# The first y0: two adjacency rows as whole fp32 products, scaled in the accumulators

## What is computed

```python
def _L0_gnn_ref(x, adj, weight, bias):
    y = jnp.einsum('nm,bmf->bnf', adj, x)
    y = y + x
    y = jnp.einsum('bnf,fo->bno', y, weight) + bias
    norm = jnp.sqrt(jnp.sum(y * y, axis=2, keepdims=True))
    return y / jnp.maximum(norm, 1e-12)
...
x = _layernorm(x + _L0_gnn_ref(x, adj, ...), axis=-1)
x = _layernorm(x + _L1_gnn_ref(x, adj, ...), axis=-1)   # masked attention
x = _layernorm(x + _L2_gnn_ref(x, adj, ...), axis=-1)   # gated relation layer
x = _layernorm(x + _L3_gnn_ref(x, adj, ...), axis=-1)   # Chebyshev layer
```

## Time and profile before

| | |
|---|---|
| median of three timed executions | 658.12 us |
| the profiled execution: its own time | 658.38 us |
| its span, first to last instruction | 656.2 us |
| TensorE busy | 629.6 us (96%) |
| VectorE busy | 567.4 us (86%) |
| ScalarE busy | 400.3 us (61%) |
| GpSimd busy | 74.1 us (11%) |
| mean granted TensorE clock | 0.996 of full |

### The profile page before, as it was taken

One profiled execution on the slowest core, in us unless ns is written; L12 is line 12 of the kernel. 1 busy time (PEld: TensorE's weight loads), 2 busy tenths in 40 slices (PEclk: granted clock), 3 DMA queues, 4 the chain that ended last, 5 costly groups with the idle time before them and its releaser, 6 DMA issues.

```text
span 656.2 us, 17523 instructions
## 1 busy us (share of the span) xinstructions
PE 629.6 (96%) x7443; PEld 487.4 (74%) x7443; DVE 567.4 (86%) x1512; ACT 400.3 (61%) x706; POOL 74.1 (11%) x50
## 2 busy tenths in 40 slices
PE   8899989999999999999999999999999999889994
PEld 3456767698678966799667976689667986549894
DVE  6889597889998999889899899889898898989635
ACT  6979572455946579274964659365893649432522
POOL 0114010020003100210002200021002100020002
PEclk9999999999999999999999999999999999999998
DMA  8710000000000200002000200002000000000012
GB/s 337 260 65 2 1 1 1 1 34 2 2 2 1 66 2 1 1 2 66 2 1 1 67 1 1 2 3 66 1 1 2 17 19 1 1 1 2 2 34 65
DMA packets 12445, 18.74 MB, mean 29 GB/s; under 512 B 592, under 2 KB 9040, under 8 KB 12368
## 3 DMA queue, kind: packets, MB, share of 16 engines
q1 hardware_dynamic: 12368, 17.63, 8.1%
HBM read 13.44 MB, written 4.19 MB: 27 GB/s over the span
## 4 chain that ended last, share of the span: by engine, by line
PE 62%; DVE 23%; ACT 7%; issue 4%; POOL 1%; DMA 1%; SPq 0%; ACTq 0%; DVEq 0%; POOLq 0%
PE r L1304 13%; PE r L1306 13%; PE r L1305 13%; DVE att L901 4%; PE r L1352 4%; DVE p_lo L906 4%; ACT att L412 3%; PE av L1467 3%; DVE stats L582 2%; PE r L1310 2%; ACT p_hi L291 2%; PE av L1476 2%; PE m L1304 2%; PE m L1305 2%; PE m L1306 2%
## 5 line engine op out<-in xcount | busy, mean ns | idle before, releaser
L248 POOL TENSOR_TENSOR small<-small,minus_half 128x8 f32<-128x8 f32 (+1 forms) x40 | 69.0, 1729 | 570.3 <-DVE small L609 308.9
L901 DVE TENSOR_TENSOR att<-att,adjT 128x1024 f32<-128x1024 f32 x64 | 77.9, 1219 | 11.3 <-ACT att L414 11.2
L412 ACT ACTIVATE att<-r,coef 128x1024 f32<-128x1024 f32 x64 | 70.4, 1101 | 21.5 <-PE r L1306 20.9
L1304 PE MATMUL r<-xq,a_hi 128*128 128x128 f16 x448 | 76.0, 219 | 0.0
L1305 PE MATMUL r<-xq,a_hi 128*128 128x128 f16 x448 | 76.0, 219 | 0.0
L1306 PE MATMUL r<-xq,a_lo 128*128 128x128 f16 x448 | 76.0, 219 | 0.0
L1304 PE MATMUL r<-rs,a_hi 128*128 128x128 f16 x448 | 75.9, 219 | 0.0
L1305 PE MATMUL r<-rs,a_hi 128*128 128x128 f16 x448 | 75.8, 219 | 0.0
L1306 PE MATMUL r<-rs,a_lo 128*128 128x128 f16 x448 | 75.8, 219 | 0.0
L414 ACT ACTIVATE att<-att 128x1024 f32<-128x1024 f32 x64 | 67.7, 1057 | 2.0
L906 DVE SCALAR_TENSOR_TENSOR p_lo<-p_hi,att 128x1024 f16<-128x1024 f16 x48 | 58.4, 1219 | 0.0
(11 more groups left out here) (423 smaller groups left out, 2110.7 us busy)
## 6 DMA issues: line engine op xcount, KB each, us to landing
adjT<-in_adj_t SPq DMA_DIRECT2D x8, 512.0 KB, 8.5
x<-in_x SPq DMA_DIRECT2D x7, 512.0 KB, 4.8
out<-outb SPq DMA_DIRECT2D x7, 512.0 KB, 3.4
pq<-in_adj SPq DMA_DIRECT2D x2, 512.0 KB, 8.6
u<-in_adj SPq DMA_DIRECT2D x2, 512.0 KB, 10.1
tmp<-in_adj SPq DMA_DIRECT2D x2, 512.0 KB, 10.5
x2s<-in_adj SPq DMA_DIRECT2D x2, 512.0 KB, 9.7
outb<-in_x SPq DMA_DIRECT2D x1, 512.0 KB, 11.8
```

What stands on the lines that cost most here:

```text
L248: return nc.gpsimd.tensor_tensor(dst, src, minus_half[:, 0:src.shape[-1]], ALU.pow)
L412: nc.scalar.activation(att[:, s], dst[:], ACT.Tanh, scale=c_tanh).then_inc(S["th"], 1)
L901: tt(att[:, s], att[:, s], adjT[:, t, :], ALU.mult).then_inc(S["pm"], 1)
L1304: mm(dst, s_hi, m_hi, start=start, stop=False, skip_group_check=True)
```

## The change

- TensorE multiplies chunks 0 and 1 (`RAW = 2`) as whole fp32 products of the unscaled features `x0` and `adjT`, four matmuls of 128 x 512 into `r1`, as soon as the chunks have landed. They stand where ten `keep_busy` products stood.
- The sum in `r1` is then multiplied in place by `x_up` = `xinv` x `ADJ_UP`: half 0 by ScalarE, half 1 by VectorE. The loop goes on with chunks 2 to 7 as before and adds the identity products of chunks 0 to 2 at chunk 2.
- The fp16 parts of chunks 0 and 1 are still needed later. GpSimd scales `adjT[0]` and `adjT[1]` in place by `ADJ_UP`, then makes `a_lo[0]` and `a_lo[1]` by a subtraction. ScalarE makes `a_hi[0]` first as before and `a_hi[1]` after chunk 7. `loop_blocks` on TensorE waits for GpSimd's two low parts.
- The transfer of the first weights goes behind chunk 2 instead of chunk 0. The product of q and k moves from chunk 1 to chunk 3, its copy on ScalarE from chunk 2 to chunk 4, `first_max` from chunk 4 to 5, `weights_sum` from chunk 6 to 7, and `x0_max(1)` behind `y0_lo`. ScalarE makes `y0_hi` before `scale_adj`, and scales chunks 0 and 1 later, behind batch 1's first `y0_hi`.

```diff
+RAW = 2
...
             for c in range(C):
                 sp.dma_start(adjT[:, c, :], adj_t[chunk(c)]).then_inc(adj_in[c], 16)
-                if c == 0:
+                if c == RAW:
                     sp.dma_start(xas[1][:, 0:4], w_first).then_inc(S["wq_in"], 16)
...
+            pool.wait_ge(S["raw_mm"], 2)
+            pool.wait_ge(S["adj_hi"], 1)
+            for c in range(RAW):
+                nc.gpsimd.tensor_scalar(adjT[:, c], adjT[:, c], ADJ_UP, None, ALU.mult).then_inc(S["adj_s"], 1)
+            for c in range(RAW):
+                pool.wait_ge(S["adj_s"], c + 1)
+                pool.wait_ge(S["adj_hi"], 1 if c == 0 else C + 1)
+                nc.gpsimd.tensor_tensor(a_lo[:, c], adjT[:, c], a_hi[:, c], ALU.subtract).then_inc(S["adj_lo_p"], 1)
...
-            for c in range(C):
+            def row_hi(c):
                 act.wait_ge(adj_in[c], 16)
+                copy(a_hi[:, c], adjT[:, c], ADJ_UP).then_inc(S["adj_hi"], 1)
+
+            row_hi(0)
+            first_x0_hi(0)
+            first_x0_hi(1)
+            for c in range(RAW, C):
                 if c < C - 1:
-                    copy(a_hi[:, c], adjT[:, c], ADJ_UP).then_inc(S["adj_hi"], 1)
+                    row_hi(c)
                 else:
+                    act.wait_ge(adj_in[c], 16)
                     for h in range(2):
                         copy(a_hi[:, c, half(h)], adjT[:, c, half(h)], ADJ_UP).then_inc(S["adj_hi"], 1)
-                if c < 2:
-                    first_x0_hi(c)
-                if c == 2:
+                    act.wait_ge(S["adj_s"], RAW)
+                    copy(a_hi[:, 1], adjT[:, 1]).then_inc(S["adj_hi"], 1)
+                if c == RAW:
+                    act.wait_ge(S["raw_mm"], 1)
+                    act.wait_ge(S["x_up"], 1)
+                    copy(r1[:, half(0)], r1[:, half(0)], x_up[:]).then_inc(S["raw_a"], 1)
+                if c == 4:
                     act.wait_ge(S["m_mm"], 1)
                     copy(m_sb, m7[:, 2 * P:3 * P]).then_inc(S["m_cp"], 1)
...
                 for c in range(first, last_):
-                    act.wait_ge(S["adj_lo"], c + 1 if c < C - 1 else C + 1)
-                    copy(adjT[:, c], adjT[:, c], LO_UP * P_UP).then_inc(S["adj_up"], 1)
+                    if c < RAW:
+                        act.wait_ge(S["adj_lo_p"], c + 1)
+                    else:
+                        act.wait_ge(S["adj_lo"], c + 1 - RAW if c < C - 1 else C + 1 - RAW)
+                    copy(adjT[:, c], adjT[:, c], LO_UP * P_UP / (ADJ_UP if c < RAW else 1.0)).then_inc(S["adj_up"], 1)
...
-                scale_adj(0, 3)
                 y0_hi(0, 0, r1[:, half(0)])
                 y0_hi(0, 1, r1[:, half(1)])
+                scale_adj(RAW, 3)
                 degrees(0, 3)
...
                 y0_hi(1, 0, m7[:])
+                scale_adj(0, RAW)
                 norm(0, 0, xas[0], V_CHUNKS)
...
+            dve.wait_ge(S["x_st"], 5)
+            ts(x_up[:], xinv[:], ADJ_UP, None, ALU.mult).then_inc(S["x_up"], 1)
...
-            for c in range(C):
+            first_x0_lo(0)
+            first_x0_lo(1)
+            dve.wait_ge(S["raw_mm"], 2)
+            dve.wait_ge(S["x_up"], 1)
+            ts(r1[:, half(1)], r1[:, half(1)], x_up[:], None, ALU.mult).then_inc(S["raw_d"], 1)
+            for c in range(RAW, C):
                 parts = [slice(0, N)] if c < C - 1 else [half(0), half(1)]
                 for n_, part in enumerate(parts):
-                    dve.wait_ge(S["adj_hi"], c + 1 + n_)
+                    dve.wait_ge(S["adj_hi"], c + n_)
                     stt(a_lo[:, c, part], adjT[:, c, part], ADJ_UP, a_hi[:, c, part], ALU.mult,
                         ALU.subtract).then_inc(S["adj_lo"], 1)
-                if c < 2:
-                    first_x0_lo(c)
-                if c == 4:
+                if c == 5:
                     first_max()
...
-                x0_max(1)
                 weights_split(0)
                 rows = Rows(0)
                 rows.begin()
                 y0_lo(0, 0, r1[:, half(0)])
                 y0_lo(0, 1, r1[:, half(1)])
+                x0_max(1)
                 dve.wait_ge(S["bc_in"], 16)
                 rows.y_half(0, r1[:])
...
             keep_busy(9)
             pe.wait_ge(S["x_max"], 1)
             mm(m7[:, 4:5], ones[:], xmax[:], start=True, stop=True).then_inc(S["x_sum"], 1)
-            pe.wait_ge(S["ident_ok"], 3)
-            keep_busy(10)
+            pe.wait_ge(S["x0_in"], 16)
+            for c in range(RAW):
+                pe.wait_ge(adj_in[c], 16)
+                for h in range(2):
+                    l_ = mm(r1[:, half(h)], x0[:, c], adjT[:, c, half(h)], start=(c == 0), stop=(c == RAW - 1))
+                    if c == RAW - 1:
+                        l_.then_inc(S["raw_mm"], 1)
...
             def loop_blocks():
 
+                pe.wait_ge(S["adj_lo_p"], RAW)
                 for h in range(2):
...
-            for c in range(C):
-                if c == 1:
+            pe.wait_ge(S["iu_ok"], 1)
+            for c in range(RAW, C):
+                if c == 3:
                     pe.wait_ge(S["wq_in"], 16)
                     pe.wait_ge(S["x_st"], 1)
                     mm(m7[:, 2 * P:3 * P], qT, kT, start=True, stop=True).then_inc(S["m_mm"], 1)
-                if c == 6:
+                if c == C - 1:
                     weights_sum(0, 0, 3)
-                if c in (0, C // 2):
-                    pe.wait_ge(S["x_lo"], 1 + 2 * c // C)
-                for h in range(2):
+                if c in (RAW, C // 2):
+                    pe.wait_ge(S["x_lo"], 1 + c // (C // 2))
+                for h in range(2):
+                    if c == RAW:
+                        pe.wait_ge(S[("raw_a", "raw_d")[h]], 1)
                     if h == 0 or c == C - 1:
-                        pe.wait_ge(S["adj_lo"], c + h + 1)
+                        pe.wait_ge(S["adj_lo"], c + h + 1 - RAW)
                     l_ = split_product(r1[:, half(h)], x0s[:, 0, c], x0s[:, 1, c], a_hi[:, c, half(h)], a_lo[:, c, half(h)],
-                                       c == 0, c == C - 1)
+                                       False, c == C - 1)
                     if c // (C // 2) == h:
-                        for part in range(2):
-                            l_ = mm(r1[:, chunk(c)], x0s[:, part, c], ident_up[:], start=False, stop=False, skip_group_check=True)
+                        for m in range(0 if c == RAW else c, c + 1):
+                            for part in range(2):
+                                l_ = mm(r1[:, chunk(m)], x0s[:, part, m], ident_up[:], start=False, stop=False, skip_group_check=True)
                     if c == C - 1:
                         l_.then_inc(S["y0_mm"], 1)
```

More of the change, by code:

```diff
@@ L159, in cd @@
             return ap.rearrange("p (c d) -> p c d", c=C)
+        x_up = sb("x_up", [P, 1])
         z_all = Stage(x3, xq, rs, pq, u, outb, r0)
@@ L164, in adj_resnorm @@
         names = ("w_in bc_in wq_in iu_ok x_in x1_in ident_ok const_ok m_cp w3_c m_mm w_max w_sum w_red w_ok wj_c "
-                 "dg_mm dg_hi dg_lo adj_hi adj_lo adj_up deg_ok sc_ok b3_ok "
+                 "dg_mm dg_hi dg_lo adj_hi adj_lo adj_lo_p adj_s adj_up raw_mm raw_a raw_d x_up deg_ok sc_ok b3_ok "
                  "norm_sq norm_r dis_ok x0_in x_max x_sum x_st x_hi x_lo "
```

## The result

The changed kernel takes 662.77 us (median of five executions, 662.35 to 665.67) against 658.12 for the kernel before on the same chip: a ratio of 1.0079, 95% interval 1.0057 to 1.0101. It is slower, inside the range, and 0.8 us less so than the 663.6 forecast. The profiled execution took 662.35 us, its span 659.8: the span grew by 3.6 us, what lies around it from 2.2 to 2.55.

A forecast was written before the change was run, and what follows sets the result against it. The bound was when VectorE begins y_half(0), at 23.69 us. GpSimd holding up VectorE's low parts was to delay it 5.45 us: 658.38 + 5.45 = 663.8 profiled, median 0.26 lower, 663.6 us; range 657.5 to 667.

The forecast's parts named there:

- The size of the hold: GpSimd beside VectorE's low parts: scaling 1.3 us, subtraction 2.4 us, each blocking throughout, together 7.4 us, between 5.5 and 10.
- with 10 it is +8: Upper bound: 10 us of GpSimd work beside VectorE's low parts would delay y_half(0) by 8 us.
- The walk: Timeline from chunk arrival to y_half(0), GpSimd and VectorE locking each other out both ways: y_half(0) at 29.15, +5.45 us.
- +0.15 without interference: Walk to y_half(0) with GpSimd not disturbing VectorE: start at 23.85 us, +0.15, TensorE's gain eaten by the later weights' sum.
- the mark: Start of VectorE's y_half(0), 23.69 us in the kernel before; whatever moves it was said to move all behind it.
- ScalarE costs nothing: ScalarE's two scalings before batch 0's norm, 1.97 us, fill 1.59 us idle; the 0.3 too much costs nothing.
- nothing gives the loss back: After y_half(0), the 5.45 us delay was to stay to the end, since TensorE is full behind 40 us.
- 29.5 when TensorE comes there: loop_blocks on TensorE: GpSimd's low parts done at 21.9 us, TensorE said to reach it at 29.5.
- Rival 1 (no lock): GpSimd beside VectorE's low parts costs little: +0.15 us, at most +1.3, 658.3, not slower; chance 0.28 shared with Rival 4.
- Rival 2 (no backlog): VectorE's last low part ends right after ScalarE's last copy, 18.0 instead of 19.05: -0.5 to -1.4, 657.2; chance 0.10.
- Rival 3: As forecast, but gaps in TensorE's loop drop its clock to 1.2 GHz, or GpSimd at upper bound: +8, 666.2; chance 0.14.
- Rival 4: Raw products hold TensorE past low part 2, ending after 11.2 us; time as in Rival 1, chance 0.28 shared with it.

The follow-up runs named there:

- before_with_gpsimd_reads: Kernel before plus two scalings and two subtractions on GpSimd, on buffers nobody reads, and two memsets filling these at the start; 664.95 us.
- memsets and filler: Changed kernel with two GpSimd memsets in place of its scalings and subtractions, and nine keep_busy products between raw products and loop; 659.14 us.
- memsets and no filler: Changed kernel with two GpSimd memsets of a_lo[0] and a_lo[1] (zeros) in place of its scalings and subtractions; 660.6 us.
- order_only: Kernel before with only the moves of the transfer, q and k product and copy, first_max, weights_sum and x0_max(1); 658.69 us.
- gpsimd_late: Changed kernel with GpSimd's four instructions waiting for VectorE's last low part and a_hi[1] behind y0_hi; 665.49 us.
- subtractions_behind_y0_lo: Changed kernel plus nine keep_busy products, ScalarE scaling chunks 0 and 1, copy and weights_sum moved, GpSimd only subtracting, after the first y0_lo; 660.2 us.
- subtractions_behind_split: Changed kernel plus nine keep_busy products, ScalarE scaling chunks 0 and 1, copy and weights_sum moved, GpSimd only subtracting, after the first weights' split; 658.6 us.
- before_with_four_scalings: Kernel before plus four idle GpSimd scalings of 128x1024 beside VectorE's low parts, on buffers nobody reads, no subtraction; 661.65 us.

## Why the prediction came out as it did

**Direction and mechanism: right.** GpSimd's instructions and VectorE's two-operand low parts keep each other out, in both directions. What was inferred from the roots' 2.54 against 1.64 us held for the direction that the trace before didn't show, as before_with_gpsimd_reads shows with no other engine's program changed. In both directions the one that comes second waits for the first: GpSimd through VectorE's instruction, VectorE through a part of GpSimd's.

**The size of the hold: the term that was off.** Predicted: scaling 1.3 us and subtraction 2.4 us, blocked for their whole length, 7.4 us in all. Measured: the scaling is much longer (2.8 us) and blocks much less (0.85 us, from when VectorE's instruction of that moment is over), the subtraction blocks 1.93 of its 2.12 us; 5.56 in all. The rule "blocked until the first has finished", which the prediction took from the Trainium skill, "SBUF — State Buffer", Who interferes with whom, holds for the subtraction to 0.2 us and not for the scaling. Had it held with the true lengths (2 x 2.8 + 2 x 2.12 = 9.8 us), the price would have been some 7.8 us by the prediction's own line ("with 10 it is +8"). Two errors in the scaling, length and share, partly cancelled: that is luck.

**The walk.** Low parts: predicted to end at 24.25, measured 23.26; the weights' sum read at 24.9, measured 23.18; `y_half(0)` at 29.15, measured 27.32. Of the 1.83 us between them, 1.0 is the earlier end of the low parts, most of it the shorter hold. Another 0.7 is that TensorE had the weights' sum (21.60) before the last low part: since subtraction 1 fell on the first half of part 7, and not on part 6, chunk 6 was through early. Part of the difference came back in the median by what the walk didn't have: 0.35 us more around the span, and a lower mean clock in some executions (0.993, 0.993 and 0.989 where the time is 662.8, 662.9 and 665.7, against 0.995 in the profiled one). So the median is 4.65 us behind, the span 3.6, and that the forecast of +5.45 came within 0.8 us of the median is in part luck.

**"+0.15 without interference": too low.** With memsets and filler the mark is at +1.15. Most of the 1.0 us between is the start of the loop: chunk 2 begins at 12.59 where the walk had 11.7, 0.7 of it because the raw products began at 1.2 GHz; the prediction had taken 2.4 GHz for all of them. (With memsets and no filler they ran at 2.4 GHz and chunk 2 began at 11.67, as walked, but then the loop itself ran at 1.2 GHz.) The second missing term is on ScalarE: the q and k copy behind chunk 4 waits for TensorE, and the high part of chunk 5 stands behind it. It shows as a gap of 0.24 us in TensorE's loop, before chunk 6 at 18.89, and as 0.3 us at the last low part in order_only. The prediction looked at what waits for the product, not at what queues behind the waiting copy. In the changed kernel low part 5 waits 0.34 us for the same reason.

**Behind the mark.** "ScalarE costs nothing" and "nothing gives the loss back" were right: 3.63 at the mark, 3.64 at the scores, 3.6 at the end. But "29.5 when TensorE comes there" for `loop_blocks` was wrong. TensorE begins them at 24.27 in the kernel before and at 28.38 in the changed one; it did no harm here, with GpSimd done at 22.11. The same mistake spoiled the expectation for gpsimd_late, and it cost 1.5 us between mark and scores in subtractions_behind_y0_lo, the lower clock included.

**Rival 1 (no lock)** is out: the low parts grow by up to 1.92 us. **Rival 2 (no backlog)** is nearly what subtractions_behind_split does, at no gain. **Rival 3**: by the mean clocks it may stand behind the 0.4, 0.6 and 3.3 us by which three executions lie above the fastest, but the profiled one doesn't show it (1.00 in all windows of 2 us read from 12 to 36 us). **Rival 4** is out: half 1 of the raw sum is read at 10.13.

## What to carry to other kernels

An idle engine isn't free help: before moving streaming work to GpSimd, list what VectorE runs beside it, and put the work where VectorE reads PSUM or one fp32 operand in a reduction, not beside instructions with two SBUF operands or a `tensor_scalar` from SBUF of more than one column; even a memset held such a `tensor_scalar` up. Then check who waits for the result and what stands behind that wait on its engine: moved late, the same two instructions cost 3 us and moved right, nothing. When an engine on the path is relieved, read from the trace how near the next one is; here VectorE got 1 us ahead of ScalarE and TensorE, and the time stayed the same.

## What the runs showed of the hardware

- A GpSimd `tensor_scalar` over 128x1024 fp32 takes 2.8 us and keeps a two-operand VectorE instruction out for 0.84 to 0.89 us; a `tensor_tensor` takes 2.12 and keeps it out for 1.93. If VectorE is in a low part when GpSimd starts, GpSimd waits for its end first (3.02 to 3.60 us for 2.8) and the hold counts from there. That the one with fewer operands is the longer was not expected. The Trainium skill, "GPSIMD Engine Reference", Performance versus the Vector engine, has 2.6 cycles an element for two inputs, an estimate of 2.2 us that the 2.12 bears out, and 1.03 for a body of up to two operations, an estimate of 0.9 us, a third of the 2.8 measured for the scaling, though near the time for which it holds VectorE.
- VectorE's `tensor_scalar` 128x128 fp32 to fp16 from SBUF is held too (1.90 for 0.28 us), also one of 128x3 (0.81 for 0.17, four scalings) and a `pair` of 128x16 with two operands (1.02 for 0.18 in gpsimd_late). A reduction of 128x1024 fp32 from SBUF (1.21) and instructions with a PSUM operand (0.69, 0.74) are not.
- GpSimd memsets of 128x1024 take 0.95 us and hold no low part up (1.21 us beside them). They do hold VectorE's `tensor_scalar` 128x128 up: `ident_up` takes 1.94 us in before_with_gpsimd_reads and 1.05 in before_with_four_scalings, where it is 0.23 without them.
- Kernels with GpSimd's large instructions show 2.2 to 2.7 us around the span where the kernel before and order_only have 2.1 to 2.2; those with memsets alone are among them (2.3 to 2.6). The cause is open.
- Two executions of eleven of the last kernel have 2.4 us more at the same mean clock (0.996) as the others. The kernel before has a few that are 1 to 1.8 us above its median, also at 0.996 or 0.997. They weren't profiled, and stay unexplained.
